# A graph network kernel: GpSimd's first gather waits for the out-degree histogram

## The reference

```python
# layer 0
m = relu(x[src] + edge_feat)
x = layernorm(x + (1 + eps) * x + segment_sum(m, dst))
# layer 1
deg = bincount(src, length=n)              # the histogram
ci = rsqrt(max(out_deg, 1)); h = where(in_deg > 0, agg * cj, x)
x = layernorm(x + relu(h @ W.T + b))
# layer 2 (also by src, with deg), layer 3 (edge network, sums by src, layernorm)
```

## Time and profile before

| | |
|---|---|
| median of 3 runs | 2671.24 us (2667.08 to 2674.76) |
| span of the profiled execution | 3047.5 us |
| the profiled execution's own time | the page gives none besides its span |
| busy in it: VectorE | 1926.7 us (63%) |
| busy: GpSimd | 1858.8 us (61%) |
| busy: TensorE / ScalarE | 633.7 us (21%) / 632.0 us (21%) |

### The profile page before, as it was taken

How to read it: one execution, slowest core, us unless ns; L and a number is a source line. 1 busy time by engine, 2 the same in 40 slices (tenths; PEclk the granted TensorE clock), 3 DMA queues, 4 the chain that set the end, 5 groups by cost and what they waited for, 6 DMA issues and landing times.

```text
span 3047.5 us, 12805 instructions
## 1 busy us (share of the span) xinstructions
PE 633.7 (21%) x2848; PEld 506.5 (17%) x2848; DVE 1926.7 (63%) x2735; ACT 632.0 (21%) x1121; POOL 1858.8 (61%) x1768
## 2 busy tenths in 40 slices
PE   1111600000028875554422100001430000000000
PEld 0000300000028765443422100001330000000000
DVE  2001799999717766754623825997349999948872
ACT  1001800222113332211211101322112223221110
POOL 4774002777766664556175757777556676574776
PEclk8555955555555555666555555555555555555555
DMA  3110086787014433322860193443122223110000
GB/s 118 22 22 13 1 323 231 257 322 269 16 34 142 142 125 103 86 53 55 49 46 13 18 71 114 130 137 119 50 59 72 87 69 103 58 41 9 17 16 15
DMA packets 158467, 276.20 MB, mean 91 GB/s; under 512 B 88601, under 2 KB 113507, under 8 KB 158259
## 3 DMA queue, kind: packets, MB, share of 16 engines
q1 hardware_dynamic: 96675, 206.39, 24.0%
q0 software_dynamic: 56448, 44.23, 8.7%
q10 hardware_dynamic: 5264, 24.74, 2.2%
HBM read 142.41 MB, written 138.17 MB: 92 GB/s over the span
## 4 chain that ended last, share of the span: by engine, by line
DVE 27%; POOL 22%; issue 16%; another core or an unknown queue 12%; PE 8%; DMA 8%; ACT 7%; SPq 0%; ACTq 0%; DVEq 0%; POOLq 0%
POOL XD L470 7%; POOL out L507 7%; POOL x_table L507 3%; POOL ring L457 3%; PE psT L883 2%; DMA din<-x_table 2%; DMA din<-in_xaux 2%; POOL x_with_degree L507 2%; DVE du L1345 2%; DVE var L1351 2%; DVE psS L1342 2%; DVE do L1362 2%; DMA xa_table<-din 2%; DVE sumb L1270 2%
## 5 line engine op out<-in xcount | busy, mean ns | idle before, releaser
L470 POOL DMA_INDIRECT XD<-xa_table,dstI x196 | 222.1, 1133 | 290.5 <-SPq L360 231.0
L507 POOL DMA_INDIRECT x_table<-sumb,put x196 | 212.6, 1085 | 154.7 <-ACT sumb L619 86.5
L457 POOL DMA_INDIRECT ring<-x_with_degree,srcI x196 | 208.2, 1062 | 146.0 <-DVEq L1426 85.1
L592 ACT ACTIVATE sq<-du 128x1344 f32<-128x1344 f32 x129 | 168.9, 1321 | 536.7 <-DVE du L1345 416.5
L457 POOL DMA_INDIRECT ring<-h_by_src,zs x196 | 214.6, 1095 | 104.0 <-issue 63.5
L457 POOL DMA_INDIRECT ring<-x_table,srcI x196 | 199.5, 1018 | 121.1 <-issue 63.2
L507 POOL DMA_INDIRECT x_with_degree<-sumb,put x196 | 209.6, 1070 | 94.0 <-issue 58.1
L507 POOL DMA_INDIRECT out<-sumb,put x196 | 201.9, 1030 | 94.9 <-issue 60.9
L457 POOL DMA_INDIRECT ring<-edge_records,dstI x196 | 202.2, 1032 | 86.8 <-issue 57.6
L470 POOL DMA_INDIRECT XD<-in_xaux,srcI x196 | 187.7, 958 | 87.9 <-issue 60.3
L1240 DVE TENSOR_SCALAR GX<-GX 128x784 bf16<-128x784 int16 x196 | 74.7, 426 | 253.3 <-remote 204.1
(11 more groups left out here) (322 smaller groups left out, 2907.4 us busy)
## 6 DMA issues: line engine op xcount, KB each, us to landing
din<-in_xaux SPq DMA_DIRECT2D x56, 728.0 KB
xa_table<-din SPq DMA_DIRECT2D x28, 728.0 KB
x_table<-GX SPq DMA_DIRECT2D x28, 686.0 KB
x_with_degree<-GX SPq DMA_DIRECT2D x28, 686.0 KB
din<-x_table SPq DMA_DIRECT2D x28, 686.0 KB
x_table<-do SPq DMA_DIRECT2D x28, 672.0 KB
din<-x_table SPq DMA_DIRECT2D x28, 672.0 KB
out<-do SPq DMA_DIRECT2D x28, 672.0 KB
```

Source lines behind the costliest of these rows:

```text
L457: pool.indirect_dma_start(ring[:, h, t, 0:w], None, table, bass.IndirectOffsetOnAxis(ap=of[:, c * H + t:c * H + t + 1], axis=0), **skip).t ...
L470: pool.indirect_dma_start(XD[:, t, 0:w], None, table, bass.IndirectOffsetOnAxis(ap=of[:, t:t + 1], axis=0)).then_inc(rows[c].sem, rows[c]. ...
L507: pool.indirect_dma_start(table, bass.IndirectOffsetOnAxis(ap=put[:, c * H + t:c * H + t + 1], axis=0), rows_of[:, h, t, :], None, bounds_ ...
L592: nc.scalar.activation(sq[:, h, :, :], u, ACT.Square).then_inc(S["squared"], 1)
```

## The change

GpSimd waits for `counted` to reach CE + 4 = 200 before its first gather. `counted` starts at 4 and has 200 when TensorE has finished column 196. Nothing else is changed.

```diff
             with pool.If(unsorted != 0):
                 sort_edges()
             pool.wait_ge(edges.sem, edges.up(5))
+            pool.wait_ge(S["counted"], CE + 4)
             gather_in_place(A["xaux"], XW, srcI)
             pool.wait_ge(S["xa_done"], 1)
             gather_in_place(XA, XW, dstI, xs_free)
```

## The result

The changed kernel takes 2772.66 us (median of 4, 2769.07 to 2774.67), the kernel before 2671.51 us (median of 4 runs): ratio 1.0384, interval 1.0366 to 1.0401, +101.2 us. The forecast was 2773.

A forecast was written before the change was run, and what follows sets the result against it. GpSimd's queue of gathers and scatters was taken to carry the end. 0 on the histogram and +102 on gather 2's start, nothing absorbing it: 2671 + 102 = 2773 us, range 2742 to 2804 (2690 to 2812 with a partly real delay).

The forecast's parts named there:

- The histogram's time in the runs compared: TensorE's histogram before the change: 196 columns at 0.46 us from 38.3, ending at 128.5 in runs, without the trace's delay.
- Rival (a): Histogram: the trace is true, runs have the 5.6 us columns too; gather 2 starts 111 us earlier, 2560; chance 0.10.
- rival (b): Histogram: DVE's compares and GpSimd's gathers exclude each other, 245 us of columns; 28 us faster, 2643; chance 0.03.
- The table: Table pass between histogram and gather 2: ends 141 us after the histogram, at 270 in runs.
- Gather 1 before: GpSimd's gather by source before the change: ends at 276 to 294, taken as 294, when gather 2 starts.
- Gather 1 after: GpSimd's gather by source after the change: starts at 129, pace 1.37, ends at 396; gather 2 starts +102 us.
- Rival (c): Part of the delay is real, histogram to 166 to 245: gather 2's start +10 to +70, 2681 to 2741; chance 0.08.
- Nothing behind it absorbs the delay: After gather 2's start: a fixed amount of work follows, so its +102 us passes whole to the end.
- VectorE's room: Dense pass before gather 2's end: over at 516 against 576, so VectorE has some 60 us to spare.
- my third point: Against the slow histogram in runs: the 231 us wait plus 165 us unknown make 396, against the 376 missing.
- The profiled execution after: Whole profiled span after the change: some 2918 to 2950 us, 100 to 130 shorter, while runs get longer.
- work isn't late, only TensorE's message: Slow histogram columns in the trace: each increment of `counted` arrives some 22 us after its matmul.

The follow-up runs named there:

- e11_dve_late: Kernel before, VectorE waiting for chunk 9 of gather 1 ahead of its first edge chunk, machine without the delay: 2694.6 us against 2672.1, ratio 1.0084.
- e10_half: Kernel before, GpSimd waiting for half of the histogram columns ahead of gather 1, machine without the delay: 2726.7 us against 2672.1, ratio 1.0203.
- e7_twice: Kernel before with two more matmuls per histogram column, into a bank nothing reads, machine with the delay: 3099.5 us against 3056.2, ratio 1.0131.
- e6_full: The changed kernel unaltered, against the kernel before on one chip with the delay: 3142.1 us against 3056.2, ratio 1.026.
- e9_paced: Kernel before, GpSimd waiting for each of gather 1's first 28 DMAs to land, machine with the delay: 3019.9 us against 3041.1.

## Why the prediction was right, and where it wasn't

- **Luck.** The forecast in us assumes a machine on which the kernel before takes 2671, and the result came from such a machine. On a machine with the delay, where four of the five sets of experiments fell, the changed kernel takes 3142 and loses 86 us by another path, the sort.
- **The histogram's time in the runs compared.** Taken as 38.3 to 128.5; in every trace without the delay it comes out within 3 us: it ends at 128.8 in the changed kernel and at 131.4 in e11_dve_late beside gather 1 at full rate. Rival (a) is false there, and rival (b) too: beside gathers the compare has its median of 420 ns and the histogram takes 92 us, not 245. The Trainium skill, SBUF — State Buffer, section SBUF: two separate sides, lets the two block each other for a whole instruction. The trace shows little of it for this compare: a mean of 433 ns and a longest of 672 beside gathers (e11_dve_late), 420 and 427 without (the changed kernel).
- **The table.** 141 us was too short: with gathers beside it, xa_done comes 150 us after the histogram in the changed kernel (278.9 - 128.8), and at 285.6 + 2.3 = 287.9 in e11_dve_late, 157 us after it. That changed nothing, since gather 1 ended at about the same time (last start 285.9; GpSimd waited 1.2 us). But the two ends are nearly level there. Going by the 294.3 of the next point, some 6 us lay between them in the kernel before, where I had 24: a table pass longer by more than that would have eaten into the loss.
- **Gather 1 before.** Taken to end at 294. No trace of the unaltered kernel without the delay was had; 395.5 - 101.2 = 294.3 is what the loss implies, and e11_dve_late, where VectorE rested through part of it, has 287.
- **Gather 1 after.** 396 expected, gather 2 started at 395.5. Two small errors cancel: gather 1 began at 131.2 for 129, and went a little faster than the 1.37 I took (1.349 on the whole). That the +102 came out to 1 us is in part this. The dense pass began at 411.8 for 411.
- **Rival (c)'s price.** Its two ends are worked out with different ends of gather 1, 396 for the +10 and 378 for the +70. With 396 for both it is +10 to +89, which overlaps the forecast's range from +71. No run depended on it.
- **Nothing behind it absorbs the delay.** Confirmed by the doses on machines without the delay: a start 0, 57.6 and 102.1 us later costs 0, 54.6 and 101.2 us.
- **VectorE's room.** 60 us was wrong by about 20. I compared the end of the dense pass with the end of gather 2, and left out the first rows that must be updated and staged before the scatter; it didn't count, as VectorE was no later than gather 2.
- **The cause of the trace's delay.** "I take the slow histogram as something the recording causes", and that runs don't have it, failed as put. Three chips gave medians of 3041 to 3059 us in plain repetition, and the changed kernel, e10_half and e11_dve_late were recorded without any delay. The right half was that the runs to be compared didn't have it, and that rested on 2671 against 3047. That trace and runs came from machines in different condition is what I should have offered as a case: the sum of my third point closes for that as well as for a recording that causes the delay. What the condition is stays open. The delay was seen where TensorE or VectorE had short instructions to do beside gathers at full rate. It let one through per 1.4 us (5.6 / 4, 11.2 / 8, 2.83 / 2), whatever the instruction (e7_twice, e6_full), and it depends on the gathers' rate (e9_paced). That would fit records which the chip writes for each instruction, but no run here shows a record, and the recorded executions on machines without the delay show that recording alone doesn't bring it about. The Trainium skill, NOTIFIC — the notification-queue block, section Overflow: three behaviours, one of which stalls the engine, lets the block that writes records hold back an engine. Whether it does so here is not shown.
- **The profiled execution after.** 2918 to 2950 was forecast, 2768.9 came on a machine without the delay, 3158.2 on one with it. The step that failed is "work isn't late, only TensorE's message": I didn't ask who else would be beside the gathers once they were moved. It was the sort.

So the change loses on both kinds of machine. It loses 3.8% where gather 1 was free beside the histogram. It loses 2.6% (1.9 to 3.3) where gather 2 starts 123 us sooner but VectorE's edge phase starts 230 us sooner and takes 353 us more, so that the first scatter starts 97 us later (883.7 against 786.8). No version here beats both kernels where the kernel before takes 2672; e9_paced is 1% below the kernel before on a machine with the delay.

## What to carry to other kernels

When a profile's span and the runs' times differ by more than a few per cent, settle first which waits both have, and whether they come from the same machine; the waits without a releaser, summed along the chain, are the candidates. A queue of transfers in strict order on one engine, with no wait from its first entry on, passes nearly every microsecond of a late start through to the end (here 101.2 of 102.1). And when work is moved away from what it seems to collide with, look at what it will lie beside next.

## What the runs showed of the hardware that was not expected

- The same kernel takes 2672 us on one chip and 3041, 3056 (3055 in a second set of runs) and 3059 us on three others, with the same instruction durations (medians: the compare about 420 ns, an indirect DMA 944 to 948 ns) and only the messages late.
- There, beside gathers at one per 1.27 us, TensorE's increments came at 1.4 us per instruction, by my estimate some 22 us behind the work (four columns of 5.6 us); beside one per 3.2 us they weren't late at all.
- GpSimd's gathers go at 1.26 to 1.27 us beside a VectorE that hardly works, 1.32 to 1.44 beside a busy one. But in e6_full gather 2 needs (653.8 - 384.7)/195 = 1.38 us with VectorE mostly waiting (busy 75.7 of the 271 us from 384 to 655), so VectorE's busy share, by which I had read the earlier trace rows, isn't the whole reason.
